# Contracting over the 12 live rows of each 32-row strip in the outer-product matmuls of a fused four-layer kernel

## What is computed

```python
x0 = jnp.einsum('bnc,c->bn', xf, w1) + b1[0]
x1 = jnp.einsum('bnc,c->bn', xf, w2) + b2[0]
x2 = jnp.einsum('bnc,c->bn', xf, w3) + b3[0]
sim = x0[:, :, None] * x1[:, None, :]          # (B, 4096, 4096)
sm = jax.nn.softmax(sim, axis=1)
feats = jnp.einsum('bn,bnm->bm', x2, sm)
gate = jax.nn.sigmoid(feats).reshape(b, h, w, 1)
return gate * x
```

## Time and profile before

| | before |
|---|---|
| median of three runs | 5443.1 us |
| the profiled execution | 5439.41 us |
| its span, first to last instruction | 5437.6 us |
| TensorE matmuls busy | 5072.3 us (93%) |
| VectorE busy | 4387.4 us (81%) |
| ScalarE busy | 4036.2 us (74%) |
| GpSimd busy | 1966.0 us (36%) |
| granted TensorE clock, mean | 0.975 of full |

### The profile page before, as it was taken

One profiled execution on the slowest core, in us unless ns is written; L12 is line 12 of the kernel. 1 busy time (PEld: TensorE's weight loads), 2 busy tenths in 40 slices (PEclk: granted clock), 3 DMA queues, 4 the chain that ended last, 5 costly groups with the idle time before them and its releaser, 6 DMA issues.

```text
span 5437.6 us, 109580 instructions
## 1 busy us (share of the span) xinstructions
PE 5072.3 (93%) x42984; PEld 2685.9 (49%) x42984; DVE 4387.4 (81%) x9218; ACT 4036.2 (74%) x6279; POOL 1966.0 (36%) x1594
## 2 busy tenths in 40 slices
PE   7799999999999999999999999999999999999986
PEld 3436445363553645446464553645446464453624
DVE  8478787887878888797887978888798887978836
ACT  1477878778786877868778786787868778786795
POOL 4225143352523425243351523425244351433403
PEclk9899999999999999999999999999999999999998
DMA  2010201102021020211102021020211102011000
GB/s 75 26 41 12 76 27 55 43 6 81 21 71 32 21 69 15 74 29 44 51 9 79 24 66 36 21 67 17 71 32 39 55 11 77 25 61 39 13 32 32
DMA packets 167965, 227.84 MB, mean 42 GB/s; under 512 B 13792, under 2 KB 146656, under 8 KB 167456
## 3 DMA queue, kind: packets, MB, share of 16 engines
q1 hardware_dynamic: 142880, 153.70, 8.5%
q0 software_dynamic: 24576, 67.14, 4.3%
HBM read 153.55 MB, written 67.24 MB: 41 GB/s over the span
## 4 chain that ended last, share of the span: by engine, by line
PE 71%; DVE 13%; ACT 10%; issue 4%; POOL 1%; DMA 0%; DVEq 0%; SPq 0%; ACTq 0%; POOLq 0%
PE PS L1239 37%; PE PS L1416 12%; PE PS L1407 5%; PE PS L1350 3%; PE PS L1515 2%; ACT big L618 2%; PE PS L1273 2%; ACT n_x L551 2%; DVE work L896 2%; PE PS L1297 2%; DVE stats L878 2%; ACT soft L618 1%; PE PS L1316 1%; DVE idx L902 1%; PE PS L1365 1%
## 5 line engine op out<-in xcount | busy, mean ns | idle before, releaser
L618 ACT ACTIVATE big<-PS 128x1024 f32<-128x1024 f32 x1216 | 1207.3, 1028 | 361.2 <-PE PS L1407 327.1
L441 POOL DMA_INDIRECT quant_H<-emb_t,idx x512 | 510.5, 997 | 905.0 <-DVE idx L902 878.4
L1239 PE MATMUL PS<-e_hi,n_hi 128*128 128x512 f16 x2048 | 780.0, 381 | 17.8 <-DVE m L896 10.1
L1239 PE MATMUL PS<-e_lo,n_hi 128*128 128x512 f16 x2048 | 776.7, 379 | 0.0
L1239 PE MATMUL PS<-e_hi,n_lo 128*128 128x512 f16 x2048 | 776.7, 379 | 0.0
L618 ACT ACTIVATE soft<-PS 128x1024 f32<-128x1024 f32 x576 | 577.5, 1030 | 254.3 <-PE PS L1407 244.8
L878 DVE BATCH_NORM_STATS2 stats<-XT 128x6 f32<-128x512 f32 x1024 | 652.9, 683 | 11.0 <-POOL XT L454 1.0
L1416 PE MATMUL PS<-big,w 128*4 128x512 f32 x4864 | 652.6, 622 | 0.0
L902 DVE FIND_INDEX8 idx<-m,work 128x8 uint32<-128x1024 f32 x512 | 624.4, 1220 | 0.0
L1407 PE MATMUL PS<-rhs,lhs 32*128 32x512 bf16 x3584 | 514.7, 395 | 80.3 <-ACT big L618 41.9
L495 POOL TENSOR_TENSOR rstd<-rstd,mhalf 128x4 f32<-128x4 f32 x128 | 132.0, 1031 | 1114.9 <-DVE rstd L1091 1114.9
(11 more groups left out here) (214 smaller groups left out, 11014.2 us busy)
## 6 DMA issues: line engine op xcount, KB each, us to landing
xin<-x SPq DMA_DIRECT2D x128, 512.0 KB, 4.3
out<-yout SPq DMA_DIRECT2D x128, 512.0 KB, 3.1
o_both<-rows_d SPq DMA_DIRECT2D x32, 512.0 KB, 7.1
quant_H<-emb_t,idx POOLq DMA_INDIRECT x512
XT<-emb SPq DMA_DIRECT2D x1, 1024.0 KB, 6.0
rows_d<-n_hi SPq DMA_DIRECT2D x32, 4.0 KB
XT<-wh SPq DMA_DIRECT2D x1, 256.0 KB, 5.6
XT<-wqv SPq DMA_DIRECT2D x1, 256.0 KB, 5.6
```

Source lines behind the costliest of these rows:

```text
L441: nc.gpsimd.indirect_dma_start(quant[:, g % 2, u, :], None, emb_t, bass.IndirectOffsetOnAxis(ap=idx[:, t % (2 * GT), 0:1], axis=0),).then_ ...
L618: nc.scalar.activation(E[h % 3][:, z * 1024:(z + 1) * 1024], bank(2 * z, 2), ACT.Exp).then_inc(exped.sem, 1)
L1239: ins = mm(dst, a, b, start=first and j == 0, stop=last and j == 2)
```

## The change

The slice of partitions over which a fill contracts is cut from 32 rows to the 12 that hold pieces. It applies to the weights (`lhs`) and to the moving tile (`rhs`). The blanking of the other 20 rows, the transposes that lay the pieces out, the outputs, the waits and the order of the steps stay as they are.

```diff
                 for r in range(2 * z, 2 * z + 2):
-                    rr = slice(32 * r, 32 * r + 32)
+                    rr = slice(32 * r, 32 * r + PIECES)
                     ins = mm(bank(r), lhs[rr, t * P:(t + 1) * P], rhs[rr, f * GW:(f + 1) * GW], start=True, stop=True)
                 ins.then_inc(filled.sem, 1)
```

## The result

The changed kernel takes 5469.75 us (median of six runs, 5461.26 to 5484.18) against 5443.89 us (5439.41 to 5453.58) beside it: ratio 1.0051, 95% interval 1.0037 to 1.0065, some 26 us more. I had forecast 5442.5 us and a range of 5433 to 5452 us. The profiled execution of after took 5467.99 us, 28.6 us over that of before.

The account below looks back on a forecast made before the run. TensorE was taken as the bound, matmuls busy 93% of the span and 71% of the chain. Stream 0, load -1.2 us and latency 0, with half the load term, gave 5442.5 us from the 5443.1 us median; range 5433 to 5452 us.

Parts of the forecast that it names:

- The stream: Fills' matmuls on TensorE: fewer rows make a 512-column matmul no faster; value taken 0.
- The load: Fills' weight loads on TensorE: 20 rows fewer save 1.5 ns each, 1.2 us over 824 pieces on the path.
- the slope of the earlier trace: Weight loads of 32 against 128 rows, 91 and 98 ns: 7 ns for 96 rows, 0.073 ns a row.
- rival A: Fills' strips stop running side by side: 181 to 544 us slower, about 5800 us; chance 0.04.
- C: Fills' load or drain goes by rows after all: faster, 5396 us or 5361 us; chance 0.07.
- Rival D: 12 rows are rounded up to the strip of 32: 5443 us; chance 0.84 together with the forecast.
- the sign of B: In the changed profile: mean clock under 0.965 with the lower slices in the middle of the span.
- rival B: TensorE's granted clock falls more often with fewer rows: 97 us slower, 5540 us; chance 0.04, half too small to see.
- the factor of rival B: Price of added half-clock time: half the rate, 0.5, times TensorE's 71% of the path, 0.71.

Follow-up runs that it names:

- stream kernel: Separate kernel, no edit of before: TensorE streams 512-column matmuls without a gap, in groups such as 4 x 12 (four strips of 12 rows); run once, no ratio given.
- runs with side matmuls: 8 extra matmuls an image in strips a fill leaves empty; 32-row kernel: 1.0003 ahead, 0.9992 behind; 12-row kernel: 1.0090, 1.0092, with 12-row extras 1.0097.

## Why the prediction was wrong

**What held.** The terms of the sum. The stream: 385 ns before and after. The load: 91 ns before and after, so the 1.2 us that I took from the slope of the earlier trace rows did not come, and a load of 12 rows is no shorter than one of 32. (The slope had a flaw of its own: the 128-row line of the earlier trace rows is f16 and the fills are bf16, so it was not a row of the same type, as I had called it.) The strips stay side by side, so rival A is out; neither the load nor the matmul got shorter, so C is out. Rival D, "nothing in the machine changes", is out by the clock: 0.963 is under the 0.965 that I had named as the sign of B, though the lower slices in the middle of the span, the other half of that sign, hardly show in the page's clock line.

**What failed** is the term that the sum doesn't have: it put the clock at nothing, because rival B's paragraph, which I gave 0.04 and half of that as too small to see, dismissed it. I wrote that "the fall goes with the engine standing still, not with few rows: fills have already only a quarter of the array's rows and keep full clock". The rows do not carry this. In the earlier trace rows the fills are 8.75 of 21.54 us; the remainder are mostly sums, matmuls of 128 rows, so the stretch showed only that the mixture holds the clock, not that fills alone would. And "a quarter of the array's rows" is right for one matmul only: the earlier trace rows has four of them side by side, 128 rows, and the earlier trace rows two, 64 rows. The change makes these 48 and 24. The stream kernel shows what that means: 4 x 12 and 2 x 12 rows lose full clock (0.54 and 0.55) at an unchanged busy time, 4 x 32 and 2 x 32 keep it. In the fused kernel it came to 126 us more at half clock, 26 us over the runs. A fall after standing still and a fall after few rows look alike in a trace in which both come together; the clean comparison, equal busy time with unequal rows, was not in the trace of before, and I should have called it open.

**The size.** I had priced B at twice the half-clock time, 272 us x 0.5 x 0.71 = 97 us. It came to 126 us more, and a us at half clock costs 0.24 to 0.27 us, not 0.36: 30 to 34 us. The range took in only 3 us for it. A bound from the earlier trace rows would have been at hand: had I taken half as much half-clock time again, the factor of rival B gives 272 x 0.5 x 0.36 = 49 us, and the high end near 5490 us. The price, 0.5 x 0.71, was in the rows; how much more half-clock time there would be was not, and half as much is a guess that I can make only now.

**What stays open.** The loss is a step between 24 and 16 rows, and its parts do not add: 12 rows in the halves just ahead of a fall left the half-clock time there as it was. In the kernel with 12 rows, extra matmuls made the loss two to three times as large, where with 32 rows the same ones raised the clock. About half of what they added is their own price; why the rest of it came as more half-clock time is not known. The runs with side matmuls exclude the delay of the fills and the added rows as the reason. I take it that the falls of one image shift when those of the next come, but no run here shows that. So it is shown that fewer rows in the fills lose clock, and that the lost clock is the loss; how rows and stalls together bring about each fall is not.

## What to carry to other kernels

On this chip, rows of zeros in a contraction can be worth keeping: cutting the rows of a matmul saved no time in the matmul and lowered the clock, with the busy time unchanged ahead of the fall that was looked at. It cost 0.5% here. Where a profile shows the clock falling one to three times in each round of a loop, an edit that leaves fewer array rows in use should be priced by the clock too, and the price of a us at half clock is read by setting each round's time against its half-clock time. Useless matmuls in strips that stand empty raised the clock here (0.972 to 0.977 and 0.978) and cost about what that gained: 4 us in 5445 in the better case, which its interval (0.9983 to 1.0001) does not tell from nothing.

## What the hardware showed that I had not expected

- Unbroken streams of 4 x 20 or 2 x 32 rows ran 42 us at half clock from rest; 4 x 24 rows rose. From full clock, 64 rows stayed and 48 fell. TensorE was busy for 98% or more of each window. This is one execution.
- Matmuls of 12, 16, 24 and 31 rows behave as those of 32 in time: load 91 ns, 385 ns recorded, side by side in their strips.
- The same kernel scatters with the clock: after ran from 5461 us at a mean clock of 0.966 to 5484 us at 0.959.
